# Message-passing kernel: all turns of an edge block ahead of its edge products, and the adjacency counts at the end of a step

## What is computed

```python
src, dst = edge_index
edge_feat = concatenate([x[src], x[dst], edge_attr], axis=-1)   # 21250 x (512+512+64)
h = mish(edge_feat @ W1 + b1)
messages = mish(h @ W2 + b2)                                    # 21250 x 512
agg = segment_sum(messages, dst, num_segments=1250)
u = mish(concatenate([x, agg], axis=-1) @ W3 + b3)
y = x + u @ W4 + b4                                             # then layer norm
```

## Time and profile before

| | us |
|---|---|
| median of 3 runs (1395.9 to 1404.0) | 1400.76 |
| the profiled execution | 1400.3 |
| its span, first to last instruction | 1398.5 |

### The profile page before, as it was taken

How to read it: one execution, slowest core, us unless ns; L and a number is a source line. 1 busy time by engine, 2 the same in 40 slices (tenths; PEclk the granted TensorE clock), 3 DMA queues, 4 the chain that set the end, 5 groups by cost and what they waited for, 6 DMA issues and landing times. The chain is left out here.

```text
span 1398.5 us, 18692 instructions
## 1 busy us (share of the span) xinstructions
PE 1256.6 (90%) x5872; PEld 1004.3 (72%) x5872; DVE 1027.4 (73%) x1809; ACT 854.4 (61%) x769; POOL 677.4 (48%) x475
## 2 busy tenths in 40 slices
PE   2964999999999999999999996787599896998997
PEld 2843777777777777777777774566488684887886
DVE  3222899999999999999999998344777347846345
ACT  1124999999999999999999995145433201311211
POOL 0017778888888888888888831125400000011000
PEclk9986999999999999999999998898799997999999
DMA  5768877777777777777777741368210410000001
GB/s 192 260 224 177 178 145 146 154 154 153 154 155 153 153 153 153 153 153 153 153 153 153 138 83 21 105 191 256 106 61 1 164 64 0 16 2 1 0 16 60
DMA packets 99177, 171.51 MB, mean 123 GB/s; under 512 B 34338, under 2 KB 39632, under 8 KB 99112
## 3 DMA queue, kind: packets, MB, share of 16 engines
q0 software_dynamic: 70000, 103.83, 38.4%
q1 hardware_dynamic: 26768, 62.22, 13.1%
q10 hardware_dynamic: 2344, 4.63, 0.9%
HBM read 133.34 MB, written 37.11 MB: 122 GB/s over the span
## 5 line engine op out<-in xcount | busy, mean ns | idle before, releaser
L500 POOL DMA_INDIRECT G<-q_dram,idx_all x168 | 348.4, 2074 | 57.0 <-issue 46.6
L800 PE MATMUL ps_x<-wA_hi,hT_hi 128*128 128x512 f32 x668 | 270.5, 405 | 1.3 <-DVE hT_lo L572 1.3
L800 PE MATMUL ps_x<-wA_hi,hT_lo 128*128 128x512 f32 x668 | 264.3, 396 | 0.0
L800 PE MATMUL ps_x<-wA_lo,hT_hi 128*128 128x512 f32 x668 | 264.2, 395 | 0.0
L492 POOL DMA_INDIRECT G<-p_dram,idx_all x168 | 173.7, 1034 | 147.5 <-issue 145.2
L800 PEld LDWEIGHTS ps_x<-wA_hi,hT_hi 128*128 128x128 f32 x668 | 125.7, 188 | 34.0 <-issue 1.9
L800 PEld LDWEIGHTS ps_x<-wA_hi,hT_lo 128*128 128x128 f32 x668 | 125.5, 188 | 30.3
L800 PEld LDWEIGHTS ps_x<-wA_lo,hT_hi 128*128 128x128 f32 x668 | 125.5, 188 | 28.5
L579 DVE TENSOR_TENSOR x<-ps_x,b 128x512 f32<-128x512 f32 x167 | 114.0, 682 | 25.8 <-PE ps_x L800 25.7
L762 PE MATMUL ps_x<-ident,G 128*128 128x128 f32 x672 | 102.4, 275 | 33.2 <-DMA G<-q_dram,idx_all 33.2
L762 PEld LDWEIGHTS ps_x<-ident,G 128*128 128x128 f32 x672 | 84.9, 142 | 56.7 <-DMA G<-q_dram,idx_all 25.1
(11 more groups left out here) (292 smaller groups left out, 2899.2 us busy)
## 6 DMA issues: line engine op xcount, KB each, us to landing
ea_raw<-in_eaT SPq DMA_DIRECT2D x84, 128.0 KB
adj_dram<-adj_sb POOLq DMA_DIRECT2D x42, 210.2 KB
adj_dram<-zeros SPq DMA_DIRECT2D x11, 640.5 KB, 4.6
adj_in<-adj_dram SPq DMA_DIRECT2D x10, 640.0 KB, 5.4
adjT_dram<-adjT_sb SPq DMA_DIRECT2D x10, 640.0 KB, 6.7
adjT_rest<-adjT_dram SPq DMA_DIRECT2D x8, 640.0 KB, 9.1
w_raw_n<-in_w SPq DMA_DIRECT2D x4, 1024.0 KB, 5.4
agg_dram<-agg_sb POOLq DMA_DIRECT2D x42, 84.0 KB
```

The costliest lines, as they stand in the source:

```text
L500: g.indirect_dma_start(G[:, b.slot, c * D:(c + 1) * D], None, q_dram, bass.IndirectOffsetOnAxis(ap=idx_all[:, i:i + 1], axis=0), compute_o ...
L800: last = t.matmul(ps_x2[c % 2][:, :], h[:, b.slot, e], w[:, k, :], start=(k == 0 and i == 0), stop=(k == KD - 1 and i == 2))
```

## The change

`first` no longer goes slice by slice: it does the 16 turns of a block, into all four banks of `ps_x1`, and then the eight edge products. Its wait for the gathered rows stands ahead of the turns as before, the waits for `h1_of` of the block before stand ahead of turns 0 and 2 of the slices, and the wait for the edge attributes stands ahead of the products. `adjacency(s-2)` goes from between `second(s, 0)` and `second(s, 1)` to the end of the step, behind `sums(s-2)`. ACT's `evac_adj` handles block s-3 instead of s-2, at the same place of its step. No instruction is added or taken away.

```diff
@@ -724,7 +724,7 @@
                     sigmoid1(s.at(1))
                     arctan1(s.at(1))
-                    evac_adj(s.at(-2))
+                    evac_adj(s.at(-3))
                     sine1(s.at(1), 0)
@@ -749,21 +749,22 @@
-                def first(b, f):
-
-                    if b.real():
-                        if f == 0:
-                            pe.wait_ge(ea_ready, b.count(1))
-                            pe.wait_ge(q_in[b.slot], b.slot_count(16 * TE))
-                        if f % 2 == 0 and b.at(-1).real():
-                            pe.wait_ge(h1_ready, b.at(-1).count(2, f // 2 + 1))
-                        out = ps_x1[:, f * BE:(f + 1) * BE]
-                        for c in range(TE):
-                            t.matmul(out[:, c * P:(c + 1) * P], G[:, b.slot, c * D + f * P:c * D + (f + 1) * P], ident[:, :],
-                                     start=(c == 0), stop=False, is_transpose=True)
-                        for i, w in enumerate((wc_hi, wc_lo)):
-                            last = t.matmul(out, w[:, f * P:(f + 1) * P], ea_parts[:, b.slot, :], start=False, stop=(i == 1))
-                        last.then_inc(pre_ready, 1)
+                def first(b):
+
+                    if b.real():
+                        pe.wait_ge(q_in[b.slot], b.slot_count(16 * TE))
+                        for f in range(KD):
+                            if f % 2 == 0 and b.at(-1).real():
+                                pe.wait_ge(h1_ready, b.at(-1).count(2, f // 2 + 1))
+                            for c in range(TE):
+                                t.matmul(ps_x1[:, f * BE + c * P:f * BE + (c + 1) * P], G[:, b.slot, c * D + f * P:c * D + (f + 1) * P], ident[:, :],
+                                         start=(c == 0), stop=False, is_transpose=True)
+                        pe.wait_ge(ea_ready, b.count(1))
+                        for f in range(KD):
+                            for i, w in enumerate((wc_hi, wc_lo)):
+                                last = t.matmul(ps_x1[:, f * BE:(f + 1) * BE], w[:, f * P:(f + 1) * P], ea_parts[:, b.slot, :],
+                                                start=False, stop=(i == 1))
+                            last.then_inc(pre_ready, 1)
@@ -802,14 +803,13 @@
                 def step(s):
-                    for f in range(KD):
-                        first(s.at(1), f)
+                    first(s.at(1))
                     second(s, 0)
-                    adjacency(s.at(-2))
                     second(s, 1)
                     second(s, 2)
                     second(s, 3)
                     sums(s.at(-2))
+                    adjacency(s.at(-2))
```

## The result

The changed kernel took 1410.92 us (median; 1409.5 to 1413.0), the kernel before 1400.35 in the same job: a ratio of 1.0085, 95% interval [1.0068, 1.0102] (the ratios come with the runs; that of the two medians would be 1.0075). The forecast was 1406.5 with a range of 1398.5 to 1413. So the change makes the kernel slower by some 10 us where I had said 6, and it lies beyond the 0.5% that I called the bound of "no change". It also lies beyond the 1404 to 1409 of the forecast itself; the wide range holds it only because rival (a) had stretched it upward. The profiled execution has a span of 1408.4 us, 9.8 above that of before (by the unrounded spans).

What follows compares the result with a forecast made beforehand. PE set the pace at 17.40 us a step; after the change a PE and DVE round through m_lo would at 17.57. 31 rounds at 0.17 (5.3) plus 0.7 at the start gave +6.0, so 1406.5 us, range 1398.5 to 1413.

Steps and rivals of the forecast that it cites:

- rival (a): Counts cost more at their new seams on PE, an idle weight load exposed: 1410 at 0.1 us, 1415 at 0.28; chance 0.22.
- Part one: Grouping the 16 turns in PE's first(): cost 0, between -0.26 and +0.1 us a step.
- Part two: Moving the adjacency counts on PE: their 0.74 us change place, PE's own round stays 17.40 us.
- The round through m_lo, the sums, the counts and second(s, 0): PE and DVE round back to m_lo: 17.57 us against PE's 17.40, so +0.17 us a step.
- Rival (b): m_lo has more room ahead of the sums on PE: round 17.48, time 1403.5, or 1401 if 17.40; chance 0.19.
- The entry of 0.38: From m_lo's end on DVE to the second product of PE's sums: 0.38 us, read in block 39.
- DVE's stretch of 8.20: DVE's work without a gap from x2_of(s, 0) to the end of m_lo half 1: 8.20 us.
- The number of steps and the ends: Edge phase, blocks 5 to 36: 31 rounds at 0.17, 5.3 us, plus 0.7 us at the start.
- The tail: End of the edge phase: last counts delay ACT's copy by at most 2.6 us, covered by up to 8.0 us.
- Rival (c): Turn changeovers on PE cost what durations say: grouping saves 0.26 us a step at most, 1397.5; chance 0.09.
- Rival (d): PE's clock gate reads 16 turns as idle, 1.2 GHz level: 3.6 us more a step, 1530; chance 0.03.

Runs made afterwards that it cites:

- e1: The kernel before with only the 16 turns grouped, the counts and ACT's copy where they were: 1398.13 us, ratio 0.9992.
- e2: The kernel before with only the counts moved behind the sums and ACT's copy for block s-3, turns slice by slice: 1409.58 us, ratio 1.0071.
- e7: The changed kernel with m_lo's second half put ahead of x2_of(s, 2) on DVE, counts still at the step's end: 1396.72 us, ratio 0.9978.
- e3: The changed kernel with the counts one place earlier, between second(s, 3) and the sums: 1396.74 us, ratio 0.9979.
- e4: The changed kernel with PE's wait for agg_evac written ahead of its wait for m_lo, in front of the sums: 1409.16 us, ratio 1.006.
- e6: The changed kernel without POOL's gather of P for each block's fourth tile, Q stored there instead of added: 1406.32 us, ratio 1.0043.

## Why the prediction was right, and where its terms were off

**Part one: 0, between -0.26 and +0.1.** Right: e1 has 0.9992 [0.9981, 1.0004]. The starts show a small gain that I had ruled out, 3.574 to 3.576 instead of 3.61, some 0.035 a step; in the changed kernel, where the counts stand ahead of the turns, it is 3.600, and 0.01 is left. Hardly any of it reaches the period: 17.394 in e1 against 17.397, and 17.70 in the changed kernel, where PE isn't the bound, against 17.72 in e2. Of the 0.034 by which e1 stays above 17.36, two single steps near the end (17.69 and 17.65) are 0.02, and sums that start 0.015 later behind second(s, 3) than in e7 are the rest; what makes the two steps long isn't traced.

**Part two, the counts 0.74.** Right: from their first start to the turns 515.76 - 515.02 = 0.74, as the earlier trace rows had it at the old place. **Rival (a)**, a dearer seam, is out as the cause by these rows and by e7, in which the counts stand at the same place and the loss is gone; what is left of it is 0.02 us a step, below the 0.03 at which it was to decide. Its time, 1410 to 1415, holds the measured 1410.9, and the forecast's own 1404 to 1409 doesn't. That the stated range held was luck in this sense: the bound that took it in came from a rival whose mechanism is all but absent.

**The round through m_lo, the sums, the counts and second(s, 0).** This is the mechanism, right in each sign that was named: PE's load released late at the sums, DVE idle before x2_of(s, 0) with 0.037 behind PE, the period beyond PE's own. Taking the counts out of it (e3) and bringing m_lo forward (e7) each take the whole loss away. **Rival (b)**, that m_lo has more room than 0.07, fell: the entry was larger than 0.38, not smaller (0.395 even without the register operation, e4).

**The terms that were mis-sized** are the first and the last of the sum, 0.08 each.
- *The entry of 0.38.* It was read in block 39, in the drain of the pipeline and in the order of before. There the product itself waited for m_lo. In the loop of the changed kernel it is 0.465; with the waits turned round (e4) it is 0.395. The register operation was in no row, since the kernel before doesn't have it there: it came with the change, and the prediction took the waits of a moved neighbour to stay as they were.
- *DVE's stretch of 8.20.* It was taken from one step, and it held in every step of the kernel before (8.19 to 8.21), where POOL's gathers hold one-hots only ahead of the stretch. The prediction named this as its weak point ("if DVE's stretch ... is not 8.20 when it starts on PE's signal"), but put no range on it. It became 8.28: with the new rhythm a one-hot of tile 2 or 3 meets the end of a gather in two steps of three, at 0.10 each. With fewer gathers it is 8.218 (e6).

**The number of steps and the ends.** 31 steps and 0.7 at the start: the excess is in the 32 from 8 to 40, with 1.4 for the eight before them, and in the drain 1.4 come back, so the ends together gave 0 and not 0.7. Measured: 32 x 0.308 = 9.85, where 31 x 0.17 + 0.7 = 6.0 had been predicted.

**The tail.** Counted as covered, and it is, but by luck of a large cover: the delay wasn't "at most 2.6". In the last rows of the edge phase, answering to the earlier trace rows:

```profile
884.94 0.52 ACT L679 COPY adj_sb<-ps_adj 128x427 f32<-128x427 f32 x1 [6.84 <-PE ps_adj L775]
...
894.08 1.21 POOL L513 DMA_DIRECT2D adj_dram<-adj_sb  x1 [9.69 <-issue]
...
904.40 0.69 DVE L667 TENSOR_TENSOR Y<-ps_x,b 128x512 f32<-128x512 f32 x1 [2.10 <-PE ps_x L840]
...
908.43 0.62 POOL L1076 DMA_DIRECT2D n_gam<-in_g  x1 [12.27 <-POOLq L455]
```

DVE's last addition ends at 905.09, 11.0 us behind the start of POOL's last window; before, with that window's start at 885.04, it was 891.52 - 885.04 = 6.5. So it came 4.5 us later in relation to the windows. What makes up the 4.5 isn't traced. Yet the next phase starts 908.43 - 894.08 = 14.35 us behind that window, and before 899.52 - 885.04 = 14.48: POOL's last window still sets it, with at most 3.3 us of cover left (908.43 - 905.09).

**Rival (c)**, that a changeover costs what the durations say, would give 17.14 for PE's round; PE's round is 17.36. **Rival (d)**, the clock gate: the turns took 1.91 us in each step of the loop, (1.91 - 0.28) / 15 = 0.109 apart with 0.28 for one, and the granted clock is 1.00 from 400 to 600 us, the 2.4 GHz level. The Trainium skill's sentence that turns don't count as activity in the same way (TensorE: Matmul & The Clock Gate, "Part 4: PE-mode transpose") is neither shown nor refuted by that: with products on both sides of the group, 16 turns did not lower the clock.

## What to carry to other kernels

In a software pipeline written out by hand, moving work within an engine's order costs next to nothing on that engine and its whole length in a round that enters it ahead of the new place and leaves behind it: write down each round with the engines it passes, and see which of them the moved work joins. Work that nobody waits for soon belongs ahead of the wait whose producer is late, not behind it; here that was one line, 14 us apart. A piece of such a round that was read while it had slack is a lower end for its length: whatever hides in slack (a short instruction held by another engine's) counts once the round is closed. And a move can change more than the order of the work: here it also turned the order of two waits. These two pieces of 0.08 us in 32 steps were about half of the loss.

## What the runs showed of the hardware

- **An operation between two waits.** A register operation between the wait for the late producer and the product costs 0.07 us in each step: the first weight load starts 0.12 behind the producer's end (the changed kernel) instead of 0.06 (e4). In these runs the order with the late wait last was the cheaper one.
- **A one-hot of 128x128 fp16 lasts up to 0.49 instead of 0.25 us** where it starts 0.32 to 0.49 us ahead of the end of a gather of POOL (of about 1 us), and both end together (within 0.007 us in the median, 30 of 120). One that starts inside a gather but 0.58 us or more ahead of its end isn't held. A held one costs the DVE stretch 0.10 us, by the starts.
- **The first edge product lasts 0.48 and a second 0.40, but the group of turns saves 0.035 us of starts in all**, not three times 0.08; with fp16 products directly ahead of the turns 0.01 is left (3.600 against 3.612).
- **Turns of 128x128 in fp32 in a row start 0.109 us apart**, 16 as well as four, at a granted clock of 1.00.
